# A mixture-of-experts stack: gate products from raw rows, and a slot table with row gathers in place of scattered rows

## What is computed

```
x = x + 0.5 * moe(LN(x));   x = x + mixer(LN(x));   x = x + 0.5 * moe(LN(x))

moe(t):  logits = t @ gate.T            # 2048 x 8
         top1 = argmax(logits);  p = softmax(logits)[top1]
         rank = how many earlier tokens chose the same expert
         tokens of rank >= 320 get nothing from this layer
         out = p * (gelu(t @ wi[top1]) @ wo[top1])   # 512 -> 2048 -> 512
```

## Time and profile before

| | |
|---|---|
| runs, median | 1186.38 us |
| the profiled execution | 1185.13 us, of which span 1183.4 us |
| PE busy | 1060.2 us, 90% of the span |
| DVE busy | 735.2 us, 62% |
| ACT busy | 564.3 us, 48% |
| POOL busy | 127.4 us, 11% |
| TensorE's mean granted clock | 0.956 |

### The profile page before, as it was taken

The page is one execution under the profiler, slowest core; times in us unless marked ns, Lnnn a source line. Parts: engine busy times, 40 slices in busy tenths (PEclk is TensorE's granted clock), DMA queues, the critical chain, the costliest instruction groups (busy, mean ns, idle before and its releaser), DMA issues.

```text
span 1183.4 us, 20868 instructions
## 1 busy us (share of the span) xinstructions
PE 1060.2 (90%) x7658; PEld 979.0 (83%) x7658; DVE 735.2 (62%) x1199; ACT 564.3 (48%) x871; POOL 127.4 (11%) x140
## 2 busy tenths in 40 slices
PE   5469999999999999399999983799999999999995
PEld 2269999999999999378778731799999999999995
DVE  6535656676576777368686743356677676765652
ACT  4335545565455656154332232345555565654441
POOL 3500101011010110100000014001011010110100
PEclk8879999999999999799999997799999999999998
DMA  9775944537375472400000023636547565472610
GB/s 281 241 254 200 356 162 169 200 129 263 123 261 193 143 250 79 134 31 1 1 36 36 36 75 142 238 116 219 200 157 259 172 225 200 149 258 92 226 60 23
DMA packets 90330, 189.05 MB, mean 160 GB/s; under 512 B 4592, under 2 KB 5104, under 8 KB 90224
## 3 DMA queue, kind: packets, MB, share of 16 engines
q1 hardware_dynamic: 84272, 169.50, 42.0%
q0 software_dynamic: 6016, 18.97, 4.2%
HBM read 160.02 MB, written 32.62 MB: 163 GB/s over the span
## 4 chain that ended last, share of the span: by engine, by line
PE 76%; DMA 8%; issue 5%; ACT 3%; POOL 3%; DVE 3%; SPq 1%; DVEq 0%; ACTq 0%; POOLq 0%
PE psH L1062 11%; PE psH L1064 11%; PE psH L1063 11%; PE acc L1069 9%; PE acc L1071 9%; PE acc L1070 9%; DMA raw_wi<-in_wi 5%; PE acc L1062 3%; PE acc L1064 3%; PE acc L1063 3%; POOL disp L456 2%; PE psT L1221 1%; PE acc L1177 1%; PE psH L1177 1%; DMA xt<-in_x 1%
## 5 line engine op out<-in xcount | busy, mean ns | idle before, releaser
L1062 PE MATMUL psH<-dth,wih 128*128 128x240 f32 (+5 forms) x1024 | 296.5, 290 | 7.7 <-issue 7.2
L1069 PE MATMUL acc<-hth,woh 128*128 128x240 f32 (+5 forms) x1024 | 294.6, 288 | 9.1 <-DVE htl L734 9.1
L1064 PE MATMUL psH<-dth,wil 128*128 128x240 f32 (+5 forms) x1024 | 294.9, 288 | 0.0
L1063 PE MATMUL psH<-dtl,wih 128*128 128x240 f32 (+5 forms) x1024 | 294.7, 288 | 0.0
L1071 PE MATMUL acc<-hth,wol 128*128 128x240 f32 (+5 forms) x1024 | 294.1, 287 | 0.0
L1070 PE MATMUL acc<-htl,woh 128*128 128x240 f32 (+5 forms) x1024 | 293.8, 287 | 0.0
L734 DVE TENSOR_TENSOR wol<-raw_wo,woh 128x1024 fp32r<-128x1024 f32 x128 | 156.3, 1223 | 133.1 <-ACT woh L576 133.0
L1062 PEld LDWEIGHTS psH<-dth,wih 128*128 128x128 f32 x1024 | 194.5, 190 | 11.6 <-issue 11.6
L576 ACT ACTIVATE woh<-raw_wo 128x1024 fp32r<-128x1024 f32 x128 | 135.4, 1059 | 144.0 <-PE acc L1071 142.0
L1069 PEld LDWEIGHTS acc<-hth,woh 128*128 128x128 f32 x1024 | 193.8, 189 | 10.6 <-DVE htl L734 10.6
L596 ACT ACTIVATE gel<-psH 128x320 f32<-128x320 f32 x256 | 111.0, 437 | 191.7 <-PE psH L1064 188.8
(11 more groups left out here) (160 smaller groups left out, 1153.9 us busy)
## 6 DMA issues: line engine op xcount, KB each, us to landing
raw_wi<-in_wi SPq DMA_DIRECT2D x64, 1024.0 KB, 6.6
raw_wo<-in_wo SPq DMA_DIRECT2D x64, 1024.0 KB, 7.8
dtok<-disp SPq DMA_DIRECT2D x16, 516.0 KB, 3.9
disp<-zeros SPq DMA_DIRECT2D x4, 1287.5 KB, 21.2
out_x<-xt SPq DMA_DIRECT2D x4, 1024.0 KB, 4.7
xt<-in_x SPq DMA_DIRECT2D x3, 1024.0 KB, 13.1
xt<-x SPq DMA_DIRECT2D x3, 1024.0 KB, 12.6
dtok<-disp SPq DMA_DIRECT2D x16, 129.0 KB, 4.2
```

What stands on the lines that cost most here:

```text
L1062: pe.matmul(out, lh, rh, start=first, stop=False)
L1063: pe.matmul(out, lh, rl, start=False, stop=False)
L1064: return pe.matmul(out, ll, rh, start=False, stop=last)
L1069: pe.matmul(out, lh, rh, start=False, stop=False, skip_group_check=True)
```

## The change

**Gate product.** PE turns the raw rows of `xt` and no longer the normed ones, two tiles at a time (`turn(p)`), and the gate weights are centred first (`gates`: each column less its mean), so that the mean of the token drops out; the factor 1/std multiplies the differences of logits in `choose`. The four chunks of 128 channels are four products of 32 output partitions each, by `tile_position` into four strips of one bank, with no accumulation (L1190 of the new file); `folds` adds the four strips by a product with a matrix of ones and turns them at once. `norm`, `norm_half` and the extra columns are gone from routing.

**Choice and rank** are made in two batches of eight tiles (`choose`, `place`). `ranks(1)` counts the tiles of batch 0 by eight more products. `take_counts` is sixteen small products.

**Slot table.** `place` writes one-hot matrices: `at_lane` (position in a chunk of 128 slots), `at_place` (expert and chunk, 24), and `at_facts`, the latter times four facts of the token (row + 1, weight, 1/std, -mean/std). PE's `tabulate` sums, over the tokens, the product of the two: a table of 128 lanes by 24 chunks by 4 facts. DVE reads source rows and target rows from it (`tables`). The 16 scatters, `disp`, its clearing and `load_tokens` are gone.

**Experts.** POOL gathers an expert's rows, by three indirect transfers, straight from x (layer 0) or the output (layer 1) into `rows[a]`, two buffers; that for expert e+2 is issued when the scatters of expert e have landed. ACT norms them (`norm_rows`, three per expert, in place of the three `xr`). DVE's `stage` in expert e waits for the gather of e+1. The result is added in place in `rows` and scattered from there.

**Order.** In the last group of the mixer PE turns pairs 0 to 2 in the loop, and the rest of the routing's PE work for layer 1 up to `folds(7)` stands between the last four `turn_conv`/`times_wu`. On DVE `choose(0)` and `place(0)` stand between the last `adds`. x is loaded by pairs of tiles; SP loads the first two units of wi and of wo right behind x.

```diff
-            def scatter(g, s):
...
-                for t in range(g * GROUP, (g + 1) * GROUP):
-                    pool.indirect_dma_start(disp[:, :], bass.IndirectOffsetOnAxis(ap=to_row[:, t:t + 1], axis=0),
-                                            xn[:, t, :], None).then_inc(s.scattered, 16)
...
+            def gather(e, a, source, s):
+                pool.wait_ge(s.src_set, e + 1)
+                pool.sem_inc(may_send, 1)
+                for k in range(CHUNKS):
+                    pool.indirect_dma_start(rows[a][:, k, :], None, source,
+                                            bass.IndirectOffsetOnAxis(ap=src_now[:, a, k:k + 1], axis=0)
+                                            ).then_inc(gathered[a][k], 16)
...
+                    if more:
+                        pool.wait_ge(s.res_out, 48 * e + 48)
+                        gather(e + 2, a, source, s)
...
+                    act.wait_ge(s.now_set, e + 1)
+                    act.wait_ge(gathered[a][k], base + 16 * h + 16)
+                    if not first:
+                        act.wait_ge(s.tokT_done, DC * e)
+                    act.activation(dn[:, k, :], rows[a][:, k, :], ACT.Identity,
+                                   bias=facts_now[:, a, k, SHIFT:SHIFT + 1],
+                                   scale=facts_now[:, a, k, RSTD:RSTD + 1]).then_inc(s.dn_done, 1)
...
+                def stage(e, h, a, sources, s=s, base=base):
+                    for k in range(CHUNKS):
+                        dve.wait_ge(gathered[1 - a][k], base + 16 * h + 16 * a + 16)
+                    q = bass.ds(CHUNKS * e + CHUNKS, CHUNKS)
+                    dve.tensor_copy(dst_now[:, 1 - a, :], dst[:, q])
+                    dve.tensor_copy(facts_now[:, 1 - a], table[:, q, :]).then_inc(s.now_set, 1)
+                    if sources:
+                        dve.tensor_copy(src_now[:, a, :], src[:, bass.ds(CHUNKS * e + 2 * CHUNKS, CHUNKS)]
+                                        ).then_inc(s.src_set, 1)
...
-                        ins = pe.matmul(ps_logitT[g % 2], small[:, GATE0 + c * E:GATE0 + (c + 1) * E],
-                                        xTt[:, g % 2, c, :], start=(c == 0), stop=(c == DC - 1))
...
+                    for c in range(DC):
+                        strip = slice(c * STRIP, (c + 1) * STRIP)
+                        ins = pe.matmul(ps_logitT[p % 2][strip, :], gates[:, c, :],
+                                        xTt[:, first:first + PAIR, c * P:(c + 1) * P],
+                                        start=True, stop=True, tile_position=(0, c * STRIP))
...
+                def folds(p, s=s):
+                    pe.wait_ge(s.lgT_copied, p + 1)
+                    if p == 0 and s is layers[0]:
+                        pe.wait_ge(fold_set, 1)
+                    b, first = divmod(PAIR * p, TB)
+                    for j in range(PAIR):
+                        ins = pe.matmul(ps_logit[b][:, first + j, :], lgT[:, p % 2, j * P:(j + 1) * P], fold[:, :],
+                                        start=True, stop=True)
+                    ins.then_inc(s.folded, 1)
...
+                def tabulate(b, s=s):
+                    for t in range(TB):
+                        if t == 0:
+                            pe.wait_ge(s.lanes_done, 2 * b + 1)
+                            pe.wait_ge(s.facts_pool, b + 1)
+                        if t == TB // 2:
+                            pe.wait_ge(s.lanes_done, 2 * b + 2)
+                            pe.wait_ge(s.facts_dve, b + 1)
+                        ins = pe.matmul(psH[0][:, 0:Q * FACTS], at_lane[b][:, t, :],
+                                        at_facts[b][:, t].rearrange("p f q -> p (f q)"),
+                                        start=(b == 0 and t == 0), stop=(b == BATCHES - 1 and t == TB - 1))
+                    ins.then_inc(s.tabled, 1)
...
+                dve.tensor_tensor(at_place[b][:, :, :], places[:, :].unsqueeze(1).to_broadcast([P, TB, Q]),
+                                  t8[:, 8, :].unsqueeze(2).to_broadcast([P, TB, Q]), ALU.is_equal
+                                  ).then_inc(s.place_done, 1)
+                for half in (low, high):
+                    dve.tensor_tensor(at_lane[b][:, half, :], lanes[:, :].unsqueeze(1).to_broadcast([P, TB // 2, P]),
+                                      t8[:, 5, half].unsqueeze(2).to_broadcast([P, TB // 2, P]),
+                                      ALU.is_equal).then_inc(s.lanes_done, 1)
+                dve.wait_ge(s.place_done, b + 1)
+                r = slice(b * TB + TB // 2, (b + 1) * TB)
+                dve.tensor_tensor(at_facts[b][:, high], at_place[b][:, high, :].unsqueeze(2).to_broadcast([P, TB // 2, FACTS, Q]),
+                                  facts[:, r, :].unsqueeze(3).to_broadcast([P, TB // 2, FACTS, Q]),
+                                  ALU.mult).then_inc(s.facts_dve, 1)
...
-                    pe.wait_ge(s.dtok_in, 32 * e + 32)
+                    pe.wait_ge(s.dn_done, CHUNKS * e + CHUNKS)
...
+                peek(1)
+                turn(3, nxt)
                 logits(0, nxt)
-                logits_by_tokens(0, nxt)
+                logits(1, nxt)
+                turn_conv(GROUPS - 1, 0)
+                times_wu(GROUPS - 1, 0)
+                logits(2, nxt)
+                folds(0, nxt)
+                logits(3, nxt)
+                folds(1, nxt)
+                peek(1)
+                turn_conv(GROUPS - 1, 1)
+                times_wu(GROUPS - 1, 1)
+                folds(2, nxt)
+                folds(3, nxt)
+                turn(4, nxt)
+                turn(5, nxt)
+                logits(4, nxt)
+                ranks(0, nxt)
+                peek(1)
+                turn_conv(GROUPS - 1, 2)
+                times_wu(GROUPS - 1, 2)
+                logits(5, nxt)
+                folds(4, nxt)
+                peek(1)
+                turn_conv(GROUPS - 1, 3)
+                times_wu(GROUPS - 1, 3)
+                turn(6, nxt)
+                folds(5, nxt)
+                turn(7, nxt)
+                logits(6, nxt)
+                logits(7, nxt)
+                folds(6, nxt)
+                folds(7, nxt)
+                peek(1)
 # ---- launch: one core; the weights that TensorE takes transposed are laid out so here ----
 def kernel(L0_attn_x, L0_attn_Wu, L0_attn_bu, L0_attn_Wv, L0_attn_bv, L0_attn_Wg1, L0_attn_bg1, L0_attn_Wg2,
```

More of the change, by code:

```diff
@@ L502, in expert @@
+                if n == 1:
+                    pool.wait_ge(s.kept, 16 * GROUPS)
+                gather(0, 0, source, s)
+                pool.wait_ge(s.dn_done, CHUNKS)
+                gather(1, 1, source, s)
+                if n == 0:
+                    pool.wait_ge(s.kept, 16 * UNITS)
+                def expert(e, a, more, s=s, source=source, target=target):
                     for i, (k, _) in enumerate(HELD):
-                        m = PARTS[k][1]
+                        m = ROWS[k]
@@ L516, in _ @@
+                for a in range(2):
+                    expert(E - 2 + a, a, False)
         @block.scalar
@@ L636, in expert @@
                             tokens(e + 1, c)
[L638 to L640 removed]
+                with act.Fori(0, E // 2 - 1) as h:
+                    for a in range(2):
+                        expert(h, a, False)
+                expert(E // 2 - 1, 0, False)
+                expert(E // 2 - 1, 1, True)
                 if n == 1:
@@ new lines, in batch_moments @@
+            def batch_moments(b, s):
+                q = slice(b * TB, (b + 1) * TB)
+                settle()
+                for t in range(b * TB, (b + 1) * TB):
+                    then(dve.bn_aggr(mv[:, t, :], row_stats[:, t % TB, :]))
+                settle()
+                then(dve.tensor_scalar(neg_mean[:, q], mv[:, q, 0], -1.0, None, ALU.mult))
+                settle()
+                dve.tensor_scalar(var[:, q], mv[:, q, 1], EPS, None, ALU.add).then_inc(s.var_done, 1)
+            each = [P, TB, E]
@@ L1155, in _ @@
-                for g in range(GROUPS):
-                    if n == 0 or g >= 1:
-                        logits(g)
-                        if g + 1 < GROUPS:
-                            turn(g + 1)
-                        logits_by_tokens(g)
-                        mark = peek(mark)
-                    if g >= 1:
-                        ranks(g - 1)
-                        if g == GROUPS - 1 or n == 1 and g == GROUPS - 2:
-                            mark = peek(mark)
-                ranks(GROUPS - 1)
@@ new lines, in _ @@
+                if n == 0:
+                    peek()
+                    for p in range(PAIRED):
+                        turn(p)
+                        if p >= 1:
+                            logits(p - 1)
+                        if p >= 2:
+                            folds(p - 2)
+                        if p in (2, 4, 6):
+                            peek()
+                    logits(PAIRED - 1)
+                    folds(PAIRED - 2)
+                    ranks(0)
```

(15 more changed lines are left out.)

691 lines of the change are left out of this document (349 added, 342 removed).

## The result

The kernel after the change takes 1147.01 us (median of 4 runs, 1143.43 to 1149.58) against 1186.25 us before (4 runs, 1182.94 to 1186.66): ratio 0.9672, 95% interval 0.9649 to 0.9696. It is 39 us faster. The profiled execution took 1143.43 us with a span of 1141.7 us, so it is the fastest of the four, and the sum of the prediction, 1138.6 us, is to be compared with it.

What follows compares the result with a forecast made beforehand. The prediction took the chain to the two first expert products as the bound: layer 0 -24.7, layer 1 -21.8, experts 0, together -46.5 on 1185.1, so 1138.6 profiled, 1140 median; forecast 1130 to 1147, 8-in-10 range 1130 to 1162.

Steps and rivals of the forecast that it cites:

- the sentence on `peek`: TensorE's jumps in routing: 3 us taken for five in layer 1, bounds 0 to 17; no cost in layer 0.
- the last copies and `ranks(0)` 1.5: Layer 0 routing, behind choose(0): exponentials, last copies and ranks(0) take 1.5 us, reaching 20.7 us.
- (b): First gather of each layer slowed beside DVE work: 0 to 1.5 us per layer, 1 us taken.
- (d): Handshakes not counted in the routing: 1 us a layer.
- (a): Waits on issue at five peek jumps in layer 1's routing: between 0 and 17 us, 3 us taken.
- so up to 882.4 the wait costs nothing: Layer 1, second expert: stage, due at 879.21, may wait for its gather until 882.4 us without delaying PE.
- (c): TensorE's clock at layer 1's first expert: loss left as it is; 2.5 us won if it stays at 2.4 GHz.
- Strips in turn: Rival: a pair's four gate-product strips run one after another, 1.8 us a pair; 1158.5 us in all; chance 0.22.
- part 2: Gate product's cost: strips side by side, 0.45 us a pair; by the skill's page, plus two drains for mode changes.
- Late gathers: Rival: experts wait for gathers, up to 0.8 us in each of 12 cases, 10 us: 1150; chance 0.08.
- Slower than before: Rival: gathers land 15.5 us after the scatters' landing, so PE loses 46.5 us or more in the experts; chance 0.03.
- Jumps: Rival: peek costs 3.4 us at each of five places in layer 1, giving 1154 us; chance 0.08.

Runs made afterwards that it cites:

- The run with both edits: Kernel after the change with layer 0's jumps and the one between the table's halves moved behind the table, and ranks(0) listed earlier: 1145.26 us, ratio 0.9658.
- the smaller delay: Kernel after the change with a needless 16-element GpSimd power between the scatters' landing and the next gathers: 1174.29 us, ratio 0.9925.
- the larger: Kernel after the change with a needless 32-element GpSimd power between the scatters' landing and the next gathers: 1204.69 us, ratio 1.0176.
- the run with the late stage and the larger delay: Kernel after the change with stage and norms later in each expert, plus the 32-element GpSimd power before the gathers: 1144.3 us, ratio 0.9650.

## Why the prediction was right, and where it was not

**Routing of layer 0, 8.9 us short.** `choose(0)` began at 20.5 us where the text had 17.5, and `place(0)` started at 28.87 us, not at 20.7. Of the first 3.0 us, 1.34 were a wait for TensorE, and the rest came with the statistics, which began at 6.1 us and not at 5 and waited 1.21 us for x. The steps that failed are two. One is the sentence on `peek`, "None in layer 0, where PE waits for DVE at each": in layer 0 TensorE did not wait for VectorE, VectorE waited for it, and two jumps cost 4.8 us, as the run without jumps in that stretch confirms (first gather 4.9 us earlier). The other is "the last copies and `ranks(0)` 1.5": TensorE's own order puts `ranks(0)` behind the seventh pair's folds, and listing it earlier moves `place(0)` by 6.1 us. The two overlap; together they move it by 8.1 us. The claim "PE is done at 21.5 us, before DVE asks" came from 1.9 us a pair; the turn, strips and folds took 2.0, but two jumps and the start at 5.45 us were not in it. The run with both edits brings `place(0)` to 20.73 us and the source rows to 34.2 us against the 33.8 of the sum, so the rest of the sum up to there was right in total, with VectorE's steps 1.5 us shorter than priced and the table 2.2 us longer.

**The table's products were undersized.** 0.17 us each was 96/512 of a long product; they took 0.39 us in layer 0, 0.36 and 0.46 in the two halves of layer 1. Most of it is the clock: the window from 30 to 42 us was granted 0.57, and I had kept the full clock for a stretch in which TensorE mostly waits. In the trace of the kernel after the two passes of such a product start 0.11 us apart each (0.22 a product) at 2.4 GHz, and 0.21 us (0.43) at 1.2 GHz. Behind `place(1)` that is 2.0 us instead of 0.7 in layer 0 and 4.0 in layer 1. In layer 1, 1.1 of it was the jump between the halves.

**The landing was undersized.** The gathers' landing was taken from the scatters, 2.9 us; in layer 0 it took 4.29, and the whole piece from the source rows to the third chunk 8.2 us against 5.5. Besides the landing, 0.9 us passed between the writing of the source rows and the first gather. Terms (b) and (d) held 2 us of that. The first gather took 1.18 us in layer 0, not 2.40, beside VectorE's splits, and 1.07 in layer 1, so of the 1.5 us that term (b) bounded at most 0.2 came.

**Routing of layer 1, right to 0.7 us, with partly cancelling errors.** The wait for `adds(11)` was seen for what it is. The timeline of the mixer's end, for the earlier trace rows:

```profile
658.15 0.88 PE L1173 MATMUL psT<-ident,xt 128*128 128x128 f32 x4 [3.12 <-DVE xt L1028]
...
673.34 1.06 PE L1173 MATMUL psT<-ident,xt 128*128 128x128 f32 x8 [1.89 <-DVE xt L1028]
```

On the old time scale (17.5 us later) the first of these is 675.6 us, which is the number in the prediction; the second is the bank of tile 9. The last `times_wu` then ended 3 us later than forecast, the steps behind it cost 4.5 us more (the table 3.3 and the landing 2.0, the ranks and counts 1.0 less), and against this stood 5 us of terms (a), (b), (d) of which the jumps used 1.1, and 2 us won earlier in the mixer, which no step of mine had.

**Experts: 0 predicted, -3.9 measured in both layers together.** The zero was a balance of two things that I had not seen. The step that failed is "so up to 882.4 the wait costs nothing": it followed VectorE's queue and not ScalarE's, where the first norm stands ahead of the `gel` that TensorE needs sooner. TensorE lost 5.2 us to that (rows above). But the kernel before lost 9.1 us in the same eight narrow experts to a wait that is gone after the change. Two rows of waits of the kernel before:

```profile
ACT wih L565 <- DMA raw_wi<-in_wi: 21.9, 10, 3.1
...
PE acc L1069 <- DVE htl L734: 9.1, 8, 1.9
```

After, the wait for `raw_wi` is 2.5 us in all. That the load of `dtok`, with its waits ahead of `load_wi` in SP's queue, caused it is the only difference in that queue, but it was argued from the listing and not run by itself. In layer 0 the gain was taken back by the third expert, 56.5 us instead of 51.7, with 3.64 us on issue at its head against 0.42. In layer 1 the five narrow experts are 3.0 us shorter together; the other 1.2 us are in the first, where the window of 20 us at its start was granted 0.91 against 0.86 before, part of what term (c) left open.

**The rivals.** "Strips in turn" was open and is closed by the trace and the run. A pair took 0.64 us and not 0.45, so by these figures the two drains of the array that part 2 names cost at most 0.2 us a pair. "Late gathers" and the forecast were not exclusive: the first cost 5 us. "Slower than before" was nearer than 3 in 100 suggests. From the landing of the scatters to that of the third gather the narrow experts took 9.8 to 11.6 us. With 11.3 to 13.4 us (the smaller delay) the kernel was still faster than before, with 15.2 to 16.2 us (the larger) slower, 1.0176. So the rival's 15.5 us was about right, though only the narrow experts paid. "Jumps" were misplaced, layer 0 instead of layer 1. The change itself works as foreseen: both first products moved by shorter routing, 37 us of the 46.5. That 1140 came as near as it did to 1147 (1143.4 profiled) is in part luck: 8.9 us missing in layer 0 stood against 3.9 us in the experts and 0.8 us at the end that no step had. The 1147.01 us lie at the upper edge of the forecast's own 1130 to 1147 and inside the range of 1130 to 1162.

## What to carry to other kernels

When a wait is priced by what is queued behind it, follow the queue of every engine that waits with it, down to the product that comes first, and for the narrowest case of the loop, not for one that was at hand. When work becomes shorter on one engine, ask whether the others' "free" instructions, a jump or a rank product listed late, are still covered. And where two engines hand over through a late transfer, try the wait a quarter of the loop later: here it cost nothing and won 6 us by the ratios.

## What the runs showed of the hardware

- Four full-precision products of 128 x 32 weights and 256 columns each, in four column strips, take 0.64 us together and 1.91 us in turn. The array changes between strips and whole products twice a pair; between strips and folds no gap above 0.1 us is seen.
- Six jumps of TensorE in a row to code that has not run took 22.9 and 21.3 us, with the hints of all but the first right ahead of them. With 4 us of other work between hint and jump they left 1.5 to 2.9 us on issue; with 6.8 us (the strips in turn) none, with 8 us 0 to 0.55. Visited from the last block to the first, they left 14.23 us. The Trainium skill, "Runtime: NRT & Kernel Launch", section "Instruction fetch mechanics", says that fetching is sequential and that a jump out of the current window waits for its page; the direction of these waits agrees; for their size the page has no number. It also says that there is no instruction cache that benefits from spatial locality. If that means that an earlier visit is not kept, the jumps would buy nothing; the run without them lost 4.7 us at the first expert and nothing at the others, so they buy one head, not six.
- Three gathers of 128 rows of 2 KB each, ahead of layer 0's experts, were issued in 1.18, 0.95 and 0.95 us and landed 3.6, 3.7 and 4.3 us after their start; of three beside the experts' traffic in a narrow expert the median took 7.1 us and the slowest 7.3.
- With `ranks(0)` early, TensorE was granted 1.2 GHz from some 24 us on, in an idle stretch of 2.67 us, and its small products took up to twice as long. The kernel after had 2.89 us of idle at the same place and kept 2.4 GHz to 30 us; the run with the late stage and the larger delay had 2.80 us there and 1.2 GHz from 24 us on. What decided was not tried.
